# Expert blocks gathered from DRAM bins in place of all eight experts per token, in a one-core GNN, Mamba and MoE kernel

## What is computed

```python
# x: (8192, 128) tokens, adj: (8192, 8192); all float32
h = relu(adj @ layernorm(x) @ gcn_w + gcn_b)
h = layernorm(h) * ln_g + ln_b
...                                  # in-projection, causal conv of 4 taps, dt, B, C
def step(hst, inp):                  # 256 channels x 16 states, over 8192 tokens
    dAt, dBut, Ct = inp
    hst = dAt * hst + dBut
    return (hst, hst @ Ct)
...
y = y * silu(z)
x = x + y @ w_out
# mixture of experts, top 1 of 8
H = gelu(layernorm(x) @ W1 + b1)     # W1: 128 x 512
probs = softmax(H @ Wg + bg)
assign = argmax(probs)
for e in range(8):
    y = H @ Wd[e] + bd[e]            # Wd[e]: 512 x 128
    out = out + where(assign == e, probs[:, e] * y, 0.0)
x = x + out
```

## Time and profile before

| | |
|---|---|
| median of 3 runs | 1839.88 us (1839.81 to 1846.79) |
| the profiled execution's own time | 1840.22 us |
| its span, first to last instruction | 1838.1 us |
| granted TensorE clock, mean | 0.944 |
| PE busy | 1648.3 us (90%) |
| PE weight load busy | 896.8 us (49%) |
| DVE busy | 1663.1 us (90%) |
| ACT busy | 829.9 us (45%) |
| POOL busy | 708.7 us (39%) |
| DMA, moved | 420.56 MB, mean 229 GB/s |

### The profile page before, as it was taken

The page is one execution under the profiler, slowest core; times in us unless marked ns, Lnnn a source line. Parts: engine busy times, 40 slices in busy tenths (PEclk is TensorE's granted clock), DMA queues, the critical chain, the costliest instruction groups (busy, mean ns, idle before and its releaser), DMA issues. The chain is left out here.

```text
span 1838.1 us, 18846 instructions
## 1 busy us (share of the span) xinstructions
PE 1648.3 (90%) x4856; PEld 896.8 (49%) x4856; DVE 1663.1 (90%) x2089; ACT 829.9 (45%) x1457; POOL 708.7 (39%) x340
## 2 busy tenths in 40 slices
PE   5999697999999999999999999999999999764668
PEld 2444243555554555455554545455555555432447
DVE  8118999999999999999989999999999999999974
ACT  3034455463636354463625454363635446362522
POOL 0003444434444344434434444444434443444431
PEclk9999898999999999999999999999999999876779
DMA  9889786766677777667676776667776676322210
GB/s 334 289 258 354 279 292 251 252 238 254 240 271 248 258 246 250 231 219 280 236 258 223 266 252 238 233 221 284 247 250 241 241 256 229 116 88 86 100 33 12
DMA packets 124749, 420.56 MB, mean 229 GB/s; under 512 B 13404, under 2 KB 22180, under 8 KB 124420
## 3 DMA queue, kind: packets, MB, share of 16 engines
q1 hardware_dynamic: 123236, 413.51, 64.1%
q10 hardware_dynamic: 1440, 6.29, 0.9%
HBM read 414.51 MB, written 5.24 MB: 228 GB/s over the span
## 5 line engine op out<-in xcount | busy, mean ns | idle before, releaser
L781 PE MATMUL ps_adj<-ring,nodes 128*128 128x512 f32 x2048 | 962.9, 611 | 31.4 <-DVE nodes L557 17.4
L355 POOL TENSOR_TENSOR h_c<-hidden,bc_ring 128x1024 f32<-128x1024 f32 x256 | 605.0, 2363 | 946.4 <-DVE inject L725 865.4
L609 DVE TENSOR_TENSOR_SCAN hidden<-decay,state,inject 128x512 f32<-128x512 f32 x512 | 627.6, 1268 | 37.2 <-POOL h_c L355 9.3
L781 PEld LDWEIGHTS ps_adj<-ring,nodes 128*128 128x128 f32 x2048 | 397.7, 196 | 490.9 <-issue 449.0
L734 PE MATMUL ps_e<-wd_parts,H_parts 128*128 128x512 f32 x1536 | 437.6, 436 | 9.8 <-DVE odd_acc L593 5.3
L734 PEld LDWEIGHTS ps_e<-wd_parts,H_parts 128*128 128x128 f32 x1536 | 299.5, 196 | 129.2 <-issue 52.5
L413 ACT ACTIVATE decay<-dt_sb,negA 128x512 f32<-128x512 f32 x512 | 340.1, 713 | 1.3 <-DVE dt_sb L637 1.0
L725 DVE TENSOR_TENSOR inject<-dtu_sb,bc_ring 128x1024 f32<-128x1024 f32 x256 | 318.2, 1243 | 15.4 <-DMA bc_ring<-bc_dram 13.2
L661 DVE TENSOR_TENSOR y_sum<-y_sum,h_c 128x1024 f32<-128x1024 f32 x224 | 301.2, 1345 | 0.5 <-POOL h_c L355 0.4
L406 ACT COPY state<-hidden 128x2 f32<-128x2 f32 x256 | 49.4, 193 | 515.5 <-DVE hidden L609 515.1
L593 DVE SCALAR_TENSOR_TENSOR out_sb<-ps_e,coef,out_sb 128x128 f32<-128x128 f32 x256 | 84.7, 331 | 31.1 <-PE ps_e L734 28.8
(11 more groups left out here) (108 smaller groups left out, 1100.7 us busy)
## 6 DMA issues: line engine op xcount, KB each, us to landing
ring<-adj SPq DMA_DIRECT2D x512, 512.0 KB, 4.2
bc_ring<-bc_dram SPq DMA_DIRECT2D x256, 512.0 KB, 4.8
nodes<-x_rows ACTq DMA_DIRECT2D x8, 512.0 KB, 12.4
x_tile<-x_cols SPq DMA_DIRECT2D x16, 256.0 KB, 5.7
out<-out_sb SPq DMA_DIRECT2D x16, 256.0 KB, 4.0
decay<-Wd ACTq DMA_DIRECT2D x1, 1024.0 KB
dt_sb<-Wd ACTq DMA_DIRECT2D x1, 1024.0 KB
bc_dram<-rows_sb SPq DMA_DIRECT2D x16, 64.0 KB
```

The costliest lines, as they stand in the source:

```text
L355: nc.gpsimd.tensor_tensor(h_c[:, s % 2], hidden[:, s % 2], over_halves(bc_ring[:, s % BC_RING, 1]), ALU.mult).then_inc(hc_ready, 1)
L609: scan = nc.vector.tensor_tensor_scan(hidden[:, s % 2, h], decay[:, s % 2, h], inject[:, h], state[:, h, s:s + 1], ALU.mult, ALU.add)
L781: last = nc.tensor.matmul(ps_adj[:, 0], nodes[:, m], ring[:, g % RING, m % GROUP], start=(m == 0), stop=(m == J - 1))
```

## The change

The experts of a token are no longer all computed. What the new code does:

- **ffn** (body i, tile i-1): the residual tile `x1` is now laid out with tokens on partitions and written into `rec`, a record of 258 floats per token: normalised row (128), x1 row (128), gate probability, token number. Mean and variance come from `bn_stats`/`bn_aggr` on DVE; ACT makes the normalised rows; PE transposes them for H.
- **rank** (PE, slot 15) and **dest** (DVE, body i, slot 0, tile i-2): prefix sums of the one-hot choice give each token's place in the bin of its expert. In slots 1 to 4 POOL scatters the four record blocks to DRAM (`bins`, L447), by an indirect DMA each.
- **batch** (body i from 4 to 16, 13 batches): DVE's `control` (slot 1, 16 instructions; 23 counted steps in the flush) picks up to four full blocks of 128 tokens with one expert each; POOL gathers the records (L406) and that expert's weights and bias (L401, 128 rows of 640 floats) by indirect DMAs; PE transposes the records, computes H anew (slots 10 and 12) and multiplies by the one expert (slot 14, 5 products of 128x128 per block, plain fp32); DVE's `finish` (slot 15) scales, adds x1; POOL scatters the rows to `out` (L411) in slots 0, 10, 11, 12 of the next body.
- **flush**: after the last body, five more batches take what is left in the bins, blocks that are not full included.
- **start**: SP writes Wd and bd as a table `wd_rows` in DRAM (16 DMAs) and clears `bins` (16.9 MB, as 96 DMAs of 128x344 floats, one behind each adjacency load of bodies -1 to 1). POOL makes constants by 13 iotas. The split of Wd, bd and w_dt into two fp32r parts is gone, and with it the `H_parts` and `low_parts` work of ACT and POOL.
- The hardware loop now holds bodies 6 to 13.

A POOL instruction per indirect DMA: 4 scatters of records, 4 gathers of records, 4 gathers of weights, 4 scatters to out, 16 per body from body 5 on.

The core of the diff:

```diff
+PICKS = 4
+FLUSH = 5
+REC = 2 * P + 2
+OUT_SLOTS = (0, 10, 11, 12)
...
+    BATCHES = TILES - 3
+    SPACE = EXPERTS * 2048
...
+            def expert_rows():
+                rows = wd_rows.ap().rearrange("(e p) (k c) -> e p k c", e=EXPERTS, k=5)
+                for e in range(EXPERTS):
+                    sp.dma_start(rows[e, :, 0:4], Wd[:, :, e]).then_inc(table_in, 16)
+                    sp.dma_start(rows[e, :, 4], bd[e:e + 1, 0].broadcast_to([P, P])).then_inc(table_in, 16)
...
+                        if isinstance(i, int) and i == -1 and g == 0:
+                            sp.wait_ge(node_ready, 8)
+                            expert_rows()
+                        if isinstance(i, int) and -1 <= i < 2:
+                            clear_bins((i + 1) * GROUPS + g)
-                    if g == GROUPS // 2 and (not isinstance(i, int) or 0 <= i - 3 < TILES):
-                        store(c, i, 1 - p)
...
+                    if late and s in OUT_SLOTS:
+                        c.wait(o_ready, -5, PICKS + 1)
+                    if scatter and s == 1:
+                        pool.wait_ge(zero_in, 16 + 16 * FILLS)
+                        c.wait(dest_step, -2, 6)
...
+                    if batch and s == 6:
+                        c.wait(scat_in, -2, 16 * BLOCKS)
+                        c.wait(o_ready, -6, PICKS + 1)
                     if mamba: ...  # h_c as before
+                    if late and s in OUT_SLOTS:
+                        scatter_out(q, OUT_SLOTS.index(s))
+                    if scatter and s in (1, 2, 3, 4):
+                        nc.gpsimd.indirect_dma_start(out=bins.ap(), out_offset=..., in_=rec[:, p, b], ...)
+                    if batch and s in (5, 8, 9):
+                        for j in {5: (0, 1), 8: (2,), 9: (3,)}[s]:
+                            gather_weights(p, j)
+                    if batch and s in (6, 7):
+                        for j in (2 * (s - 6), 2 * (s - 6) + 1):
+                            gather_rows(p, j)
...
+            for f in range(FLUSH):                    # POOL, after the bodies
+                c.wait(o_ready, -2, PICKS + 1)
+                pool.wait_ge(flush_step, 23 * f + 23)
+                c.wait(by_done, -2, PICKS)
+                if f == 0:
+                    pool.wait_ge(scat_in, 16 * BLOCKS * TILES)
+                for j in range(PICKS):
+                    gather_rows(k % 2, j)
+                for j in range(PICKS):
+                    gather_weights(k % 2, j)
+                if f:
+                    c.wait(o_ready, -1, PICKS + 1)
+                    for j in range(PICKS):
+                        scatter_out((k - 1) % 2, j)
...
+            for f in range(FLUSH + 1):                # PE, after the bodies
+                if f < FLUSH:
+                    c.landed(row_in, 0, (BATCHES + f) % 2)
+                    transpose((BATCHES + f) % 2, flush_bank(f, 0))
+                if f:
+                    c.wait(bh_ready, 0, 4)
+                    c.landed(wd_in, 0, (BATCHES + f - 1) % 2)
+                    experts((BATCHES + f - 1) % 2, flush_bank(f - 1, 1))
+                if f < FLUSH:
+                    for k in range(4):
+                        product(flush_bank(f, 1 - k % 2), [(w1_sb[:, k], bt_sb[:])]).then_inc(bh_done, 1)
...
-                    def unit():                       # PE: 96 fp32r products per tile
-                        product(ps_e[:, u % 2], [(H_parts[:, h, split_buffer(p, b), k], wd_parts[:, w, k, four]...)
-                                                 for k in range(4) for h, w in ((0, 0), (0, 1), (1, 0))])
+            def experts(r, bank):
+                for j in range(PICKS):
+                    product(bank[:, j * P:(j + 1) * P],
+                            [(H2[:, k, j * P:(j + 1) * P], wd_ring[:, r, j, k]) for k in range(4)]
+                            + [(mean, wd_ring[:, r, j, 4])]).then_inc(by_done, 1)
```

More of the change, by code:

```diff
@@ L21 @@
 BF16 = mybir.dt.bfloat16
+U32 = mybir.dt.uint32
 AX = mybir.AxisListType.X
@@ L330, in body @@
+            def body(i, p, adjacency, front, mamba, ffn, scatter, batch, late):
                 c = Count(pool, i)
                 q = 1 - p
+                for per in (1, 4, 5, 6, 16, 64):
+                    c.times_of(per)
                 for s in range(SLOTS):
-                    if front and s == 9:
-                        if mamba:
-                            c.wait(hc_ready, 0, s)
-                        c.wait(low_ready, 1, 1)
-                        nc.gpsimd.tensor_tensor(low_parts[64:72], low_raw, low_parts[64:72].bitcast(F32),
-                                                ALU.subtract).then_inc(low_split, 1)
-                        c.wait(low_split, 1, 1)
@@ new lines, in finish @@
+            def finish(c, d, r, bank):
+                c.landed(row_in, d, r)
+                c.landed(out_in, d - 2, r)
+                nc.vector.tensor_copy(out_at[:, r], got[:, r, :, REC - 1]).then_inc(o_ready, 1)
+                c.wait(by_done, d, PICKS)
+                for j in range(PICKS):
+                    nc.vector.scalar_tensor_tensor(out=o_sb[:, r, j], in0=bank[:, j * P:(j + 1) * P],
+                                                   scalar=got[:, r, j, 2 * P:2 * P + 1], in1=got[:, r, j, P:2 * P],
+                                                   op0=ALU.mult, op1=ALU.add).then_inc(o_ready, 1)
@@ L742, in bias_product, with transpose, rank, body @@
                 last.then_inc(start_p, 1)
-            def body(i, p, adjacency, front, mamba, ffn, experts):
+            def transpose(r, bank):
+                for j in range(PICKS):
+                    last = product(bank[:, j * P:(j + 1) * P], [(got[:, r, j, 0:P], ident)])
+                last.then_inc(bt_done, 1)
+            def experts(r, bank):
+                for j in range(PICKS):
+                    product(bank[:, j * P:(j + 1) * P],
+                            [(H2[:, k, j * P:(j + 1) * P], wd_ring[:, r, j, k]) for k in range(4)]
+                            + [(mean, wd_ring[:, r, j, 4])]).then_inc(by_done, 1)
+            def rank():
+                flat = cells(pick_bf[:])
+                n = BLOCKS * EXPERTS
+                nc.tensor.matmul(ps_y[:, 0, 0:n], tri[:], flat, start=True, stop=False)
+                for b in range(1, BLOCKS):
+                    nc.tensor.matmul(ps_y[:, 0, b * EXPERTS:n], ones[:], flat[:, 0:n - b * EXPERTS],
+                                     start=False, stop=(b == BLOCKS - 1))
+                product(ps_y[:, 0, n:n + EXPERTS], [(ones[:], pick_bf[:, b]) for b in range(BLOCKS)]
+                        ).then_inc(rank_done, 1)
+            def body(i, p, adjacency, front, mamba, ffn, scatter, batch, late):
                 c = Count(pe, i)
@@ L858, in _ @@
-            bodies(pe, body)
+                    if batch and s in (10, 12):
+                        if s == 10:
+                            c.wait(bt_ready, -4, 1)
+                            c.wait(o_ready, -5, PICKS + 1)
+                        for k in (s - 10, s - 9):
+                            if s == 12:
+                                c.wait(bh_ready, -4, k - 1)
+                            product(ps_e[:, 1 - k % 2], [(w1_sb[:, k], bt_sb[:])]).then_inc(bh_done, 1)
+                    if batch and s == 14:
+                        c.wait(bh_ready, -4, 4)
+                        c.landed(wd_in, -4, p)
+                        experts(p, ps_e[:, 1])
```

580 lines of the change are left out of this document (353 added, 227 removed).

## The result

The changed kernel takes 1885.6 us (median of 4 runs, 1878.4 to 1887.1), the kernel before 1839.9 beside it: a ratio of 1.0235, interval 1.0215 to 1.0254, **46 us slower**. The profiled execution took 1887.1 us, its span is 1885.3, at a mean granted clock of 0.885.

What follows compares the result with a forecast made beforehand. DVE was taken to set the body's length, so PE work removed is worth nothing by itself. Bodies -69, start +15 and end +85 sum to +31 on 1840.2 us: 1871, stated as 1870, range 1850 to 1905.

Steps and rivals of the forecast that it cites:

- C: The end, behind the last scan: 154 us where it was 69, a change of +85 us.
- A: The bodies: DVE work removed less work added, plus one loop turn written out, a change of -69 us.
- B: The start: added table and clear bytes over full DMA bandwidth, +11 us up to 146 us and +4 after, +15.
- 11.7: In a body: us of DVE time that go with combine, stretched y_sum, coef steps and the 512-wide normalising product.
- 7.7: In bodies 4 to 15: us of new DVE work per body, from ffn, dest, control and finish.
- This counts the POOL DMAs at nothing: In the bodies: indirect DMAs cost no time, covered by POOL's gap of some 2.5 us before an h_c.
- t = 1.3: On POOL: the time in us taken for one indirect DMA, between bounds of 0.37 and 2.36.
- 8t + 10 = 20.4: In the flush: us per batch, for four scatters, four gathers, landing, transposes, experts and finish; t is POOL's time per DMA.
- Rival 1: POOL and the end: DMA issue nearer 0.37 us, so the end is short; 1816 us at 0.5; chance of over 0.5% faster 0.25.
- Rival 2: In the bodies: indirect DMAs and y_sum exclude each other, each delaying DVE by 0.6 us; 1995 us, chance 0.12.
- Rival 3: POOL too slow: 2 us per DMA overfills double gaps by 3 us, y_sum waits for h_c; 1946 us, chance 0.13.
- Rival 4: In the bodies: PE stalls on late records or weights and holds front, 2 us a body; 1895 us, no chance given.

Runs made afterwards that it cites:

- e4: The kernel before, with only 32 of the 96 expert products per tile (both correction terms left out): 1824.1 us, ratio 0.9905.
- e6: The changed kernel with POOL's DMAs dealt out so that the short gaps between two h_c hold one each: 1864.4 us, ratio 1.0136.
- e7: The changed kernel with PE's 32 logit products of slot 10 behind the batch's first two hidden products instead of ahead: 1880.1 us, ratio 1.0194.
- e3: The changed kernel with the 16 table DMAs moved from the head of body -1 into body 1, clears unchanged: 1877.3 us, ratio 1.0203.
- e1: The changed kernel with one flush batch in place of five, the other four batches' rows not written: 1796.5 us, ratio to before 0.977.
- e9: The changed kernel with e2's edit, and in the flush DVE's control of batch f+1 before the finish of f-1: 1877.9 us, ratio 1.0185.
- e2: The changed kernel with the flush's row gathers of batch f+1 issued on POOL ahead of the scatters of f-1: 1887.8 us, ratio 1.0242.

## Why the prediction was right, and where it was off

Slower by the end, in spite of faster bodies, was the forecast, and it came true: 1885.6 for 1870, inside the range of 1850 to 1905, a loss of 46 us for 31. Of the three parts C has the right chain, A comes near by two errors that cancel, and B by luck.

**What bounds the kernel: right.** e4 shows that PE's work is worth nothing in a body and 12 us at the end.

**A, the bodies: -65.9 for -69, but by two sizes that cancel.** Bodies 2 and 3 fell by 11.1 and 11.0 us, where the terms gave 8.9. Bodies 4 to 15, the loop turn with them, fell by 44.0 for 50.9. In bodies 4 to 14 DVE's busy time fell by 7.3 us each (1110.0 to 1030.1 in all) where 4.0 stood. Both sides of that term were off:
- More goes than 11.7. The `y_sum` steps of body 3 are busy for 23.5 us before and 20.9 with the change, 2.6 less, where the prediction counted two stretches of 0.6. Before, three of them take 1.87 to 1.97 us (at 467.6, 489.1 and 520.0 us) for 1.22; with the change none does.
- Less comes than 7.7. In body 14 the control takes 2.8 us (1540.26 to 1543.02) for 3.6, and by the starts of its rows ffn's new steps and dest are 2.2 us for 2.8.

Against that stands idle time, 39.0 us more of it in bodies 4 to 14, which the prediction had at nothing:
- *"This counts the POOL DMAs at nothing"* is the step that failed. The limit it named, 1.25 us for two in a gap of 2.5, was nearly right, and 1.27 alone would have missed it by little; but the first of a pair takes 1.98. `y_sum` waits 18.8 us in these bodies, and e6 puts the price at 21 us.
- The batch's gelu on ACT ahead of `decay`, behind PE's logits, stood in no part of the prediction: 22.9 us of idle DVE, of which e7 gains 5.5 alone.

**B, the start: +12.3 for +15, a near size by luck.** Its mechanism, bytes over full bandwidth, failed. e3 leaves the clears where they are, moves only the 2.6 MB of tables, and has the whole of the loss back; what costs is one stall of 10.5 us behind the tables in SP's queue. The +4 put on body 0 did not come either: from the first scan to its once-per-tile product are 90.4 us, for 90.5 before.

**C, the end: +100.8 for +85, the miss.** By its own points, from the last scan's end:

| point | predicted | measured |
|---|---|---|
| batch 12 finished | 40 | 45.1 |
| first flush batch finished | 76 | 79.8 |
| three periods on | 137 | 147.6 |
| last batch finished | 146 | 156.8 |
| its rows landed | 154 | 163.6 |
| end of the run | 154 | 170.0 |

The chain is the predicted one (e1: 19.6 us a batch, e9: shorter when scatters and control leave it), and t = 1.3 was measured as 1.27. Mis-sized was the period, *"8t + 10 = 20.4"*: three of them took 67.8 us, 22.6 each, for 61.2. The first is 20.9, landing being 2.9 for 3.3 and the work on PE longer; the second (22.3) and third (24.5) stretch with PE's experts at a clock of 0.7 (6.6 and 6.0 us for the 4.5 taken from the earlier trace rows, in a window at a clock of 0.92), and the third with its records, which take 5.6 us to land. The other two pieces are batch 12, 5 us late, and POOL's drain, 6.4 us behind the landing, which no row of the kernel before could show. The points are those of one execution: in e3 and e7 batch 12 is finished 4 us later still, and the end is 175.8 and 174.8 us.

**The rivals.** *Rival 1* (cheap issue) fell: t is 1.27. Its counter-argument, that POOL's instructions all last over 1.2 us, holds for those of the bodies, not for a DMA, which occupies POOL for 0.96. *Rival 2* (DMA and `y_sum` exclude each other, 1995) had the right pair and the wrong direction: `y_sum` makes the DMA wait, by 1.0 us, and isn't stretched itself (1221 ns on average). Sixteen `y_sum` started 0.2 to 0.6 us after a DMA did and took 1.2 us all the same. *Rival 3* (t = 2, `y_sum` waits for `h_c`) came true in part: its mechanism is the 21.7 us above, at 0.9 us a gap for its 1.5, in the gaps where the first DMA meets a `y_sum`; the end went by 1.27. *Rival 4* (late records stall PE, 1895) hit a neighbour: what comes late is PE's product for ACT's gelu, not its work for front.

**Rule and row.** A scatter of 64 KB lands 2.1 us after its issue (1876.77 to 1878.9), a gather of records of 132 KB after 2.86 (1805.00 to 1807.86). The Trainium skill (DMA: Bandwidth & Descriptors, Anatomy of one DMA) gives 2.0 us and bytes over 436 GB/s, an estimate of 2.15 and 2.3: the scatter agrees, the gather is 0.6 us longer, and the median of all 72 gathers of records is 3.8. The Trainium skill (SBUF — State Buffer, SBUF: two separate sides) calls the shared ports an exclusive lock between a DVE instruction with two SBUF inputs and a GpSimd one that reads SBUF, held by whichever starts first. The trace agrees with it where `y_sum` is first (101 DMAs held), if issuing an indirect DMA counts as reading SBUF, and shows no lock where the DMA is first (the sixteen `y_sum`).

## What to carry to other kernels

Work that is hidden in the steady state has its price at the end: count how many rounds of a pipeline are left when the covering work is over, and multiply by the whole chain finish, scatter, gather, landing, compute. Before taking a piece out of such a chain, ask what it covers: e2's four scatters hid DVE's control of the same length, and only both edits together (e9) shortened the period. And when instructions are put into the gaps of an engine's queue, one per gap, at a place where they don't meet the other engine's two-input operation, was worth more here (21 us in e6) than their number or their mean length told.
